# First batch's queries in four banks, Wv's remainder ahead of the activations, and a weight load during the last sums, in a decoder layer with ternary experts

## What is computed

```python
x = x + _L0_attn_ref(_layernorm(x), Wqk, bqk, Wv, bv, Wu, bu, Wo, bo, ln_g, ln_b)
x = x + _L0_xattn_ref(_layernorm(x), itok, ctx, ctx, ctx)
x = x + _L0_ffn_ref(_layernorm(x), W_up, W_gate, W_down)
# attention: linear, 16 heads of 32
q = elu(x @ Wqk + bqk); k = q; v = silu(x @ Wv + bv); u = silu(x @ Wu + bu)
kv = einsum('bhnd,bhne->bhde', k, v); o = einsum('bhnd,bhde->bhne', q, kv)
out = (u * layernorm(o, ln_g, ln_b)) @ Wo + bo
# experts: token id chooses one of 4; each is a gated MLP, all three of its weights are ctx[e]
g = silu(h @ ctx[e].T); y = (g * (h @ ctx[e].T)) @ ctx[e].T
# feed forward: weights quantised to -1, 0, 1 times mean|W|
hidden = silu(x @ up.T) * (x @ gate.T); out = hidden @ down.T
```

## Time and profile before

| | us |
|---|---|
| median of 3 runs (684.96 to 686.34) | 686.11 |
| the profiled execution | 685.89 |
| its span in the trace | 684.1 |

### The profile page before, as it was taken

One profiled execution on the slowest core, in us unless ns is written; L12 is line 12 of the kernel. 1 busy time (PEld: TensorE's weight loads), 2 busy tenths in 40 slices (PEclk: granted clock), 3 DMA queues, 4 the chain that ended last, 5 costly groups with the idle time before them and its releaser, 6 DMA issues.

```text
span 684.1 us, 11895 instructions
## 1 busy us (share of the span) xinstructions
PE 667.0 (97%) x4498; PEld 434.5 (64%) x4498; DVE 512.2 (75%) x818; ACT 294.6 (43%) x440; POOL 211.1 (31%) x221
## 2 busy tenths in 40 slices
PE   8999999999999989999999999999999999999996
PEld 5456556556547575555556777777777777777772
DVE  6676873865755769999886987787878986776665
ACT  4475654545536344564332534342433434332331
POOL 4113713213135220000320443326343644324222
PEclk8999999999999999999999999999999999999999
DMA  7947039018215466883331111113020221101001
GB/s 195 374 148 238 1 117 252 0 61 234 74 61 183 143 209 216 243 229 84 67 55 28 28 28 28 28 28 90 1 55 2 44 73 28 28 1 62 1 1 61
DMA packets 78963, 65.00 MB, mean 95 GB/s; under 512 B 59200, under 2 KB 59200, under 8 KB 77888
## 3 DMA queue, kind: packets, MB, share of 16 engines
q1 hardware_dynamic: 76352, 55.89, 29.9%
q0 software_dynamic: 2560, 8.42, 3.5%
HBM read 42.51 MB, written 8.41 MB: 74 GB/s over the span
## 4 chain that ended last, share of the span: by engine, by line
PE 84%; DVE 7%; DMA 3%; issue 2%; ACT 1%; POOL 1%; SPq 1%; POOLq 0%; DVEq 0%; ACTq 0%
PE bank L1310 33%; PE bank L1602 28%; PE bank L1611 15%; PE bank L1303 3%; DVE region L889 3%; PE bank L1482 2%; PE bank L1468 2%; DVE late L885 1%; PE bank L1504 1%; DMA stage<-in_L_ffn_W_up_dram 1%; DMA late<-n 1%; ACT tmp L559 1%; DVE region L893 1%; DMA sorted_residual<-rows,pos 1%; DVE st L744 0%
## 5 line engine op out<-in xcount | busy, mean ns | idle before, releaser
L1602 PE MATMUL bank<-w_att,region 128*128 128x256 f16 x1024 | 127.6, 273 | 0.0
L1611 PE MATMUL bank<-region,w_moe 128*128 128x512 bf16 x512 | 120.3, 379 | 0.8 <-DVE w_moe L1220 0.8
L1602 PEld LDWEIGHTS bank<-w_att,region 128*128 128x128 bf16 x1024 | 100.1, 98 | 18.2 <-DVE tmpA L1235 0.2
L1310 PE MATMUL bank<-late,w_att 128*128 128x512 f16 x384 | 87.0, 381 | 1.4 <-DVE region L939 1.0
L1231 DVE TENSOR_TENSOR n<-bank,n 128x512 f32<-128x512 f32 x112 | 71.4, 684 | 19.0 <-PE bank L1602 17.1
L473 POOL TENSOR_TENSOR w_moe<-tmp,w_moe 128x512 f16<-128x512 f32 x30 | 39.2, 1306 | 139.0 <-ACT w_moe L709 139.0
L1611 PEld LDWEIGHTS bank<-region,w_moe 128*128 128x128 f16 x512 | 50.0, 98 | 48.8 <-DVE w_moe L1220 1.3
L702 ACT ACTIVATE n<-n,qs 128x512 f32<-128x512 f32 x64 | 44.5, 719 | 64.7 <-DVE n L1231 64.7
L1602 PE MATMUL bank<-w_att,late 128*128 128x256 f16 x512 | 66.4, 273 | 0.0
L1310 PEld LDWEIGHTS bank<-late,w_att 128*128 128x128 f16 x384 | 37.3, 99 | 44.6 <-DVE region L939 1.7
L1602 PEld LDWEIGHTS bank<-w_att,late 128*128 128x128 bf16 x512 | 50.0, 98 | 12.1
(11 more groups left out here) (171 smaller groups left out, 1073.7 us busy)
## 6 DMA issues: line engine op xcount, KB each, us to landing
stage<-in_L_ffn_W_up_dram SPq DMA_DIRECT2D x8, 1024.0 KB, 6.9
stage<-in_L_ffn_W_gate_dram SPq DMA_DIRECT2D x8, 1024.0 KB, 6.3
rows<-sorted_residual SPq DMA_DIRECT2D x16, 257.5 KB, 3.0
stage<-in_ctx_dram SPq DMA_DIRECT2D x4, 1024.0 KB
stage<-in_L_ffn_W_down_dram SPq DMA_DIRECT2D x4, 1024.0 KB
nrm<-in_L_ffn_W_down_dram SPq DMA_DIRECT2D x4, 1024.0 KB, 8.4
rows<-in_x_dram SPq DMA_DIRECT2D x1, 3072.0 KB, 16.1
rows<-in_x_dram SPq DMA_DIRECT2D x4, 256.0 KB, 3.7
```

The lines of the kernel that those rows point to most:

```text
L1310: mm = pe.matmul(dst, lhs(*step), rhs(*step), start=(start and n == 0), stop=(stop and n == len(steps) - 1))
L1602: mm = pe.matmul(wk_ps[bank][:, q * H:(q + 1) * H], w[:, c + q, k * P:(k + 1) * P], x3S_part[slot][:, h, m, k], start=(h == 0 and k == 0), ...
L1611: mm = pe.matmul(ffy_ps[t][:, :], hid[:, u, h, q, (t % 2) * P:(t % 2 + 1) * P], tern[2][:, c + q], start=(begins and q == 0 and h == 0), s ...
```

## The change

In the first batch the four query chunks get four banks, so that PE waits for none of them, and the 18 small matmuls between chunks 1 and 2 go. DVE makes Wv's remainder ahead of all four activations. PE's waits of V's first two products and of the first two transposes of k are changed to match. Seven small matmuls are put between the first transposes, and 58 in place of 46 run ahead of them. At the hand-over, the second sign pass over unit 0 moves ahead of the last tile's sum, and SP issues the next unit of W_up when that pass is done, ahead of its wait for the scatters. The small matmuls before and after the first unit's transposes become 14 and 66 in place of 52 and 16.

```diff
-    last_bank = [ps[0], ps[1], ps[2], ps[3]]
+    four_banks = [ps[0], ps[1], ps[2], ps[3]]
@@ SP
         unit(0, 2)
+        sp.wait_ge(s["sign_b"], 1)
+        unit(1, 0)
         sp.wait_ge(s["scattered"], 16 * NT)
@@
-        next_unit(0)
         for i in range(3, 6):
             next_tile(i)
@@ ACT batch
-                act.activation(tmp[:, m % 2], acc[m % 2][:, :], ACT.Exp, bias=cols[:, 0, m:m + 1]).then_inc(s["q_exp"], 1)
+                bank = four_banks[m] if first else acc[m % 2]
+                act.activation(tmp[:, m % 2], bank[:, :], ACT.Exp, bias=cols[:, 0, m:m + 1]).then_inc(s["q_exp"], 1)
@@ DVE batch
-            q_elu(b, 0)
-            q_elu(b, 1)
             if first:
                 split(1)
+                for m in range(K):
+                    q_elu(b, m, four_banks[m])
             else:
+                q_elu(b, 0)
+                q_elu(b, 1)
                 head_norm(b - 1)
-            q_elu(b, 2)
-            q_elu(b, 3)
+                q_elu(b, 2)
+                q_elu(b, 3)
@@ DVE hand-over
         last_sum(2)
+        two_signs(0, True)
         last_sum(3)
-        two_signs(0, True)
@@ PE first_norm
                 transposes(first_bank[t], lambda k: nrm[:, t, k * P:(k + 1) * P]).then_inc(s["t1_mm"], 1)
+                if t < T - 1:
+                    keep_busy(kv_ps, 7)
@@ PE batch
-                return (acc[m % 2][:, :], lambda i, j, k: w_att[:, 0, j, k, m * P:(m + 1) * P], lambda i, j, k: xT[:, i, k])
+                return ((four_banks[m] if first else acc[m % 2])[:, :], lambda i, j, k: w_att[:, 0, j, k, m * P:(m + 1) * P], lambda i, j, k: xT[:, i, k])
@@
-                keep_busy(kv_ps, 18)
@@
-                else:
+                elif not first:
                     pe.wait_ge(s["q_elu"], K * b + m - 1)
@@ V
-                    pe.wait_ge(s["q_elu"], K * b + 3 + t)
+                    pe.wait_ge(s["q_elu"], K * b + (1 if first else 3) + t)
@@ transposes of k
-                        pe.wait_ge(s["x_lo"], 3 + t)
+                        pe.wait_ge(s["q_elu"], K)
@@ PE opening and hand-over
-        keep_busy(kv_ps, 46)
+        keep_busy(kv_ps, 58)
@@
-        keep_busy(ps[0], 52)
+        keep_busy(ps[0], 14)
         unit_transposes(0, 0)
-        keep_busy(ps[0], 16)
+        keep_busy(ps[0], 66)
         unit_transposes(0, 1)
```

More of the change, by code:

```diff
@@ L933, in ctx_lo, with q_elu @@
                                      op1=ALU.subtract).then_inc(s["ctx_lo"], 1)
-        def q_elu(b, m):
+        def q_elu(b, m, bank=None):
+            bank = acc[m % 2] if bank is None else bank
             dve.wait_ge(s["q_exp"], K * b + m + 1)
@@ L938, in q_elu @@
             dve.wait_ge(s["q_clip"], K * b + m + 1)
-            dve.scalar_tensor_tensor(out=qT[:, m], in0=acc[m % 2][:, :], scalar=cols[:, 0, m:m + 1],
+            dve.scalar_tensor_tensor(out=qT[:, m], in0=bank[:, :], scalar=cols[:, 0, m:m + 1],
                                      in1=tmp[:, m % 2], op0=ALU.add, op1=ALU.max).then_inc(s["q_elu"], 1)
@@ L1053, in last_sum @@
         def last_sum(t):
-            residual(B - 1, t, last_bank)
+            residual(B - 1, t, four_banks)
             second_stats(B - 1, t)
@@ L1347, in operands @@
                 cut = slice(t * P, (t + 1) * P)
-                bank = last_bank[t] if bank_free is None else acc[t % 2]
+                bank = four_banks[t] if bank_free is None else acc[t % 2]
                 return bank[:, :], lambda i, j, k: aT[:, i, k, cut], lambda i, j, k: w_att[:, 3, j, k]
```

## The result

| | before | changed |
|---|---|---|
| median of 8 runs each | 685.62 (684.04 to 686.34) | 689.11 (686.04 to 690.49) |
| profiled execution | 685.89 | 688.76 |
| its span | 684.1 | 686.9 |

The changed kernel is slower: ratio 1.0041, interval 1.0025 to 1.0057. I had forecast 683.2, with a range to 685.5.

The account below looks back on a forecast made before the run. PE was taken to bound the kernel nearly everywhere from 13.31 us on, by its own work plus its waits. First batch -2.1 and hand-over -0.8 sum to -2.9 us: 686.1 becomes 683.2, range 682.1 to 685.5.

Parts of the forecast that it names:

- First batch, PE's steps: Opening: query chunks without a gap, V starts at 23.9 not 26.28, its third product at 29.2; gains 2.4 and 2.3 us.
- The clock part: Opening, first transposes: small matmuls keep the clock at 2.4 GHz, where it fell for 6.8 us; gain 0.9 us.
- what is late next: First batch: ScalarE's pass over W_up can start at 38.1, capping the gain at 2.2 us; 2.1 taken.
- Rival (c): Opening: W_up's or the context's landing holds the gain, first batch 0 to -1 us, 684.3 to 685.3; chance 0.12.
- Hand-over, the pass: Hand-over: moved sign pass delays the last sum 0.5 us but frees GpSimd's root; last scatter issued sooner, -0.3 us taken.
- Hand-over, the load: Hand-over: W_up's early load shares DMA engines with the last scatter, delaying its landing 0 to +0.9 us; +0.4 taken.
- Hand-over, the 0.9 gained: First expert step: VectorE's wait for W_up's load goes, so the first multiplication starts at 255.87; -0.9 us.
- Rival (b): Hand-over: load and pass cost the last tile what the load's absence gives, 0 to +0.9 us, 684.0 to 684.9; chance 0.14.
- Rival (d): Opening, ahead of the queries: clock falls in a new pause, kernel slower, 688.2 if cold for 10 us; chance 0.04.
- the better halves of (b) and (c): Parts of two rivals' chances counted as faster by over 0.2%, within a total of 0.84; their rest, within 0.2%, 0.12.

Follow-up runs that it names:

- the first experiment: The change's first-batch part alone, with the hand-over of the kernel before put back: 686.09 us, ratio 1.001.
- the tenth kernel: Kernel before plus the first-batch part and x's rest loaded in two, but without the small matmuls between the first transposes: 685.11 us, ratio 0.9995.

## Why the prediction was wrong

Two terms of the sum failed: W_up's landing as the cap of the opening's gain (2.1 us forecast, 0 to 0.4 came), and the price of the early load at the last scatter (+0.4 forecast, +3.1 came, with 1.5 us of PE at the lower clock behind it in the profile).

**First batch, PE's steps: right.** Queries without a gap, V at 23.43 (23.9 forecast), its third product at 28.8 (29.2), Wv's remainder out of the way early. The clock part was real, but only for some executions. Over the 98 executions of the kernel before beside the experiments, on three chips, 33 with a mean clock of 0.9975 or more have the median 684.75, 48 between 0.9955 and 0.9975 have 685.7, and 17 below have 686.7. The step that failed was to read one profiled execution's 6.8 us at the lower clock as the kernel's.

**First batch, "what is late next": the failing step.** I capped the gain by W_up's load, took its landing as 0.5 us behind the end of the bytes, 38.1, and kept 2.1 us. It landed at 39.1 to 39.8. The bytes end twice: the bulk at 37.6, and a last engine's share later, at 38.6 in the changed kernel and at 39.3 in the kernel before. The kernel before had shown it, had I read on past (kernel before):

```profile
38.50:39.00 0.50, 0.50 (x7) 0.50 (x6) 0.43 (x4) 0.50 (x2) 0.00 (x0) 1.00 0.06 25
```

and the changed kernel has it too:

```profile
38.00:38.50 0.50, 0.50 (x4) 0.24 (x3) 0.44 (x1) 0.00 (x0) 0.00 (x0) 1.00 0.08 29
```

So in the kernel before the load landed at about 39.8 (an estimate: 39.3 and the same 0.5), and the room that I had priced at 2.2 us was 0.5. Issued 2 us sooner, it landed little or not at all sooner: at 39.1 in the changed kernel (issued at 21.57 and not 23.82) and at 39.8 in the first experiment's (21.89). Rival (c) was right, and its price of 0 to -1 held: of 2.1 us, 0.5 to 1.2 were left at the pass's start, and 0 to 0.4 at the last sums. That last figure is no better than its scatter: the same changed kernel had this sum at 232.75 in one profile and 234.73 in another. That the gain returns once the 2 MB are out of W_up's way, and only together with the first batch's part, rests on the medians: each half alone at 1.001 and 0.9995, both at 0.9956 to 0.9969 in four measurements of three kernels on three chips.

**Hand-over, the pass: right.** The last sum comes 0.55 later against its neighbours (forecast 0.5), the last root takes 0.57 and not 1.53, the third's is held (1.41), and the last scatter is issued 0.8 sooner, 0.4 of it carried from the first batch. The 1.41 agrees with what the Trainium skill ("SBUF — State Buffer", section "Who interferes with whom") says of VectorE and GpSimd excluding each other.

**Hand-over, the load: the failing step.** I gave the load's megabyte "ends 0 and +0.9", from mean rates, with its bytes moving from 241 to 245. It cost +3.1. The total flow did run at 415 GB/s; what a mean rate hides is that the scatter has landed when its last row has. The rows did not share the engines with the load, as my half-way +0.4 supposed: none moved before 244.2, when most of the load was through, and one engine's rows then had a packet of code ahead of them as well. By the table the price is gone where the load's bytes are through when the last scatter is issued. The Trainium skill ("DMA: Bandwidth & Descriptors", section "Queues, rings and completion order") says that each engine goes round its queues a packet at a time, where a packet is a group of descriptors. The rows of this case show no such turns between load and scatter, 415 packets of the load and none of the scatters from 240.5 to 244.2; the trace does not name the single engines, so whether the load's whole share of an engine was one such group stays open.

**Hand-over, the 0.9 gained: true and worthless.** DVE's wait for W_up went, as forecast (the pass ran at 254.74, with no wait). In its place DVE waits 3.67 us for a silu that comes 3.8 us later than before.

**Rival (b) had the place and a third of the price.** I had bounded it at +0.9, and it gave 2.9 us net in the profile. Its ground, a scatter held up on GpSimd as in the 2.16 us of the earlier trace rows, is not what came: the last scatter was issued sooner.

**Rival (d) had the clock, in another place.** It looked for a fall ahead of the queries. It came behind PE's pause of 3.4 us at the hand-over, which I had not weighed, since I had let the scatter's landing move by 0.4 only. Its share is about 1.1 us of the median, with the noise said above.

**A sum:** "the better halves of (b) and (c)" make 0.83 and not 0.84, and the rest 0.13.

**Open:** how the tail's 2.0 us divide between the packet of code and the rows; why the first batch's part alone is 0.7 us above the kernel before in the median, where its profile is level; why one execution's W_gate took 6.9 us to land; and why the clock falls in some executions of one program and not in others.

## What to carry to other kernels

Before moving a load ahead of a small transfer that the next stage waits for, price the small one's landing as if it came wholly behind the load, on the engine that ends last, and look what else is queued there, not by bytes over mean rate; a part of the load, or the load much sooner, may be had at nearly no cost. When a limit is lifted and the time stays, look at the landing of the next transfer: two limits close together each make the other's removal look worthless, and only both together show. And where a program of several hundred microseconds shows one short stretch at a lower clock, collect the times by mean clock over many executions before a forecast rests on it.

## What the runs showed of the hardware

- A transfer landed 0.5 to 0.6 us after its last packet (248.48 and 249.01, 246.12 and 246.72), and that packet can be late: a share of 0.06 to 0.08 at 16 to 29 GB/s went on behind the bulk, for 0.6 us (last scatter of the kernel before) to 2.2 us (W_gate's load in the tenth kernel, last packet at 46.3).
- A megabyte issued 2.7 us ahead of a scatter of 256 KB moved its landing from between 3.3 and 3.9 us to between 6.3 and 6.8; a quarter of it, to between 3.8 and 4.0. Until 3.8 us after the third scatter's issue no row of it moved.
- A 16 KB packet of code took 0.99 to 1.06 us of one engine's time, in the five profiles in which it stood ahead of the last rows.
- PE's small transposes took 3.46 us at 1.2 GHz against 1.95 at 2.4, after a pause of 3.1 to 3.5 us, in two profiled executions of this hand-over (2.97 in a third); in the two with more small matmuls it stayed at 1.95.
- The fall of the clock in the opening comes and goes between executions of one program, and is worth about 2 us of 685 between the coldest and the warmest (686.7 against 684.75).
